# Batches 1 and 2 take the last batch's split of pairs between the engines in a state-space scan

## What is computed

```python
u = silu(conv(x) + conv_b)
delta = softplus(dt_proj_w @ dt_lo + dt_proj_b)
def step(state, xs):
    d_t, B_t, C_t, u_t = xs
    dA = jnp.exp(d_t[..., None] * A)
    state = state * dA + (d_t * u_t)[..., None] * B_t[:, None, :]
    y_t = jnp.einsum('ben,bn->be', state, C_t)
    return (state, y_t)
y = (y + D * u) * silu(z)
```

## Time and profile before

| | us |
|---|---|
| median of 3 runs | 533.96 (533.24 to 534.74) |
| profiled execution | 533.53 |
| its span | 531.8 |
| phases 0 to 3 begin | 27.9, 52.5, 79.7, 106.9 |
| phases 4 to 7 begin | 132.9, 161.2, 188.6, 219.7 |
| phases 8 to 11 begin | 249.8, 279.3, 306.9, 337.1 |
| phases 12 to 19 | 365.4 to 505.9 |

### The profile page before, as it was taken

How to read it: one execution, slowest core, us unless ns; L and a number is a source line. 1 busy time by engine, 2 the same in 40 slices (tenths; PEclk the granted TensorE clock), 3 DMA queues, 4 the chain that set the end, 5 groups by cost and what they waited for, 6 DMA issues and landing times.

```text
span 531.8 us, 9178 instructions
## 1 busy us (share of the span) xinstructions
PE 491.4 (92%) x3018; PEld 368.0 (69%) x3018; DVE 462.9 (87%) x846; ACT 380.1 (71%) x699; POOL 451.9 (85%) x327
## 2 busy tenths in 40 slices
PE   9989899998787999999999999999899999899688
PEld 5568788687676676668676777767566766676654
DVE  3799799799799999799999999798988989999852
ACT  4698848775876777866958776957868869768542
POOL 1389999959999999989999999889799898888910
PEclk9969799999999999999999999999999999999899
DMA  5595000126520001065230000077100000000001
GB/s 127 176 375 217 0 2 1 41 85 213 182 80 1 1 1 60 1 229 202 71 101 2 20 1 22 8 281 227 45 21 1 22 20 17 6 21 21 2 20 39
DMA packets 18704, 39.36 MB, mean 74 GB/s; under 512 B 5585, under 2 KB 6353, under 8 KB 18658
## 3 DMA queue, kind: packets, MB, share of 16 engines
q1 hardware_dynamic: 18658, 38.79, 21.4%
HBM read 34.33 MB, written 4.46 MB: 73 GB/s over the span
## 4 chain that ended last, share of the span: by engine, by line
PE 48%; POOL 19%; DVE 13%; ACT 10%; issue 9%; DMA 1%; DVEq 0%; SPq 0%; POOLq 0%; ACTq 0%
PE p_s L759 12%; PE p_y L781 11%; POOL state L586 9%; POOL dbu L571 7%; DVE state L1267 6%; PE p_v L814 5%; PE p_f L805 5%; PE p_tr L728 3%; PE p_v L691 2%; ACT da L1016 2%; DVE x L1216 2%; PE p_pr L703 2%; ACT pair_b L1000 1%; PE p_f L794 1%; PE p_pr L682 1%
## 5 line engine op out<-in xcount | busy, mean ns | idle before, releaser
L586 POOL TENSOR_TENSOR state<-state,c_bc 128x1024 f32<-128x1024 f32 (+1 forms) x131 | 256.7, 1970 | 21.6 <-DVE state L1267 19.2
L759 PEld LDWEIGHTS p_s<-pair_b,du_t 128*128 128x128 f32 x1072 | 140.7, 200 | 44.9 <-issue 33.4
L759 PE MATMUL p_s<-pair_b,du_t 128*128 128x128 f32 x1072 | 154.6, 287 | 16.0 <-DVE state L1267 15.8
L781 PE MATMUL p_y<-ident,state 128*128 128x128 f32 x1024 | 149.3, 276 | 0.0
L1016 ACT ACTIVATE p_s<-delta,a_neg 128x512 f32<-128x512 f32 (+1 forms) x162 | 93.7, 583 | 77.6 <-DVE state L1267 44.1
L1267 DVE TENSOR_TENSOR_SCAN state<-da,p_s 128x512 f32<-128x512 f32 (+1 forms) x116 | 134.5, 1172 | 16.0 <-PE p_s L759 13.1
L571 POOL TENSOR_TENSOR dbu<-du,pair_b 128x1024 f32<-128x1024 f32 (+1 forms) x80 | 145.3, 1819 | 0.2 <-DMA pair_b<-bc_rows 0.2
L781 PEld LDWEIGHTS p_y<-ident,state 128*128 128x128 f32 x1024 | 121.5, 144 | 23.3 <-issue 20.2
L1016 ACT ACTIVATE da<-delta,a_neg 128x512 f32<-128x512 f32 (+1 forms) x158 | 99.3, 647 | 18.5 <-DVE state L1267 18.4
L1267 DVE TENSOR_TENSOR_SCAN state<-p_s,dbu 128x512 f32<-128x512 f32 (+1 forms) x100 | 97.6, 996 | 7.6 <-POOL dbu L571 6.0
L805 PE MATMUL p_f<-u_sb,h_t 128*128 128x512 f32 x112 | 55.4, 597 | 2.4 <-DVE gw L1364 2.4
(11 more groups left out here) (175 smaller groups left out, 640.6 us busy)
## 6 DMA issues: line engine op xcount, KB each, us to landing
c_bc<-bc_rows SPq DMA_DIRECT2D x32, 512.0 KB, 5.1
pair_b<-bc_rows SPq DMA_DIRECT2D x16, 512.0 KB, 5.5
xs<-in_x SPq DMA_DIRECT2D x16, 256.0 KB, 4.6
out<-ot SPq DMA_DIRECT2D x14, 256.0 KB, 2.0
cx<-in_ctx_t SPq DMA_DIRECT2D x4, 512.0 KB, 3.8
u_sb<-in_u_w SPq DMA_DIRECT2D x1, 1024.0 KB, 14.1
v_sb<-in_v_w SPq DMA_DIRECT2D x1, 1024.0 KB, 15.6
w_in<-in_in_w_t SPq DMA_DIRECT2D x1, 384.0 KB, 4.7
```

The lines of the kernel that those rows point to most:

```text
L586: eng.tensor_tensor(pair, pair, c_bc[:, 2 * p:2 * p + 2, c0:c0 + w], ALU.mult).then_inc(po_cs, 1)
L759: mm = eng.matmul(p_s[g % BANKS][:, t * P:(t + 1) * P], du_t[:, f % 2, t, :], diagonals_of(n // 2)[:, n % 2, c0 // P + t, :], start=(t == ...
L781: mm = eng.matmul(p_y[:, t, :], slot(NS * f + n)[:, t * P:(t + 1) * P], ident[:, :], is_transpose=True, start=False, stop=(n == NS - 1 and ...
```

## The change

`POOL_SETS` gives batches 1 and 2 the set of batch 3: POOL makes dt\*u\*B of pairs 0, 2, 3, 5 and 6, and PE of pairs 1, 4 and 7, where POOL had 1, 3, 5, 7 and PE 0, 2, 4, 6. In `PAIRS_BY_DVE`, DVE multiplies by C the pairs 1 and 4 in all phases from 4 on. Before, these were the phases from 12 on, with pair 1 in phases 3 to 11 and pair 5 in phases 3, 7 and 11. In phases 1 and 2 DVE now takes pair 1, where it had none; in phase 3 it takes none, where it had pairs 1 and 5.

```diff
-POOL_SETS = [[2, 5], [1, 3, 5, 7], [1, 3, 5, 7], [0, 2, 3, 5, 6]]
+POOL_SETS = [[2, 5]] + 3 * [[0, 2, 3, 5, 6]]
...
     PAIRS_BY_DVE = [(LAST, 7)]
-    PAIRS_BY_DVE += [(f, p) for f in range(SPLIT, F) for p in (1, 4)]
-    PAIRS_BY_DVE += [(f, 1) for f in range(Q - 1, SPLIT)] + [(f, 5) for f in range(Q - 1, SPLIT, Q)]
+    PAIRS_BY_DVE += [(f, p) for f in range(Q, F) for p in (1, 4)]
+    PAIRS_BY_DVE += [(f, 1) for f in (1, 2)]
```

## The result

The changed kernel takes 545.08 us (median, 544.17 to 545.49) where the kernel before takes 533.60 us on the same chip. The ratio is 1.021 (95% interval 1.0187 to 1.0233): 11.5 us slower. The forecast was +5.8 us, 539.8 us, with a range up to 544.5.

A forecast was written before the change was run, and what follows sets the result against it. POOL was full in phases 4 and 5; PE, POOL and DVE nearly full in 6 to 11, with PE carrying the chain. Phase 6 begins 8.3 us late, phases 6 to 11 give -2.5: +5.8, 539.8 us; range 532.5 to 544.5.

The forecast's parts named there:

- the first turn: Phase 3 into 4: POOL's queue of 30.7 us starts pair 3 of phase 4 at 149.4 us, 5.5 us later.
- phases 1 and 2: DVE's added 1.37 us in each delays PE and ACT with nothing to cover it: +2.7 us, bounds 0 and +4.
- phases 6, 9, 10: Lengths set by the fullest engine: PE 28.8 us, DVE 28.6 us and DVE 28.6 us; -2.8 us.
- phases 7 and 8: Lengths set by the fullest engine: POOL 30.8 us in 7, DVE 29.4 us in 8; +0.5 us.
- phase 11: Length set by POOL at 28.1 us, two of its products being half size; -0.2 us.
- Each goes by the fullest engine: Phases 6 to 11: each lasts as long as its largest engine load, 174.3 us against 176.8 us, -2.5 us.
- Phases 12 to 19 keep their work: The phases after the changed split: work unchanged, so no cost was counted, 0 us.
- (c): Rival: longer waits drop TensorE's clock to 1.2 GHz, also in phase 8, 1.5 us a fall; 544.3 us, chance 0.19.
- The signs: POOL's queue into phase 4 lasts 30 to 31 us, DVE waits 4 or more there, phase 5 takes 28.5 or more.
- (a): Rival: PE decides in phases 6 to 11, giving 6.2 us; DVE's idle swallows early cost; 530.7 us, chance 0.14.
- (b): Rival: no difference, early costs of 2.9 and 1.4 us, gains of 4 in phases 6 to 11; 534.3, chance 0.12.
- (d): Rival: PE was no bound, so phases 6 to 11 give nothing; +8.3 us, 542.3 us, chance 0.10.

The follow-up runs named there:

- e2: Changed kernel with phases 1 to 3 as before: DVE has no C product in phases 1 and 2, pairs 1 and 5 in phase 3; 541.5 us.
- e1: Changed kernel with POOL's dt*u*B of the set's third pair moved ahead of C of pair 0, from phase 4 on; 535.9 us.
- e12: Changed kernel with POOL's C product of pair 5 only 64 of 512 columns wide in phases 3, 7 and 11; 541.1 us.
- e4: Only the change's second half: DVE's C products of the changed kernel with the old split of dt*u*B; 542.9 us.
- e7: Changed kernel with DVE's C product of pair 4 cut to 32 of 512 columns in phases 4 to 11; 540.7 us.
- e3: Only the change's first half: the new POOL sets in batches 1 and 2, with DVE's C products of before; 545.1 us.
- e11: Changed kernel with 27 extra matmuls on TensorE in phase 4 to fill its waits; 546.1 us.
- e6: Changed kernel with phases 1 to 3 as before, DVE also taking C of pair 5 in phases 7 and 11, and e1's move; 533.7 us.
- e10: e6 with DVE taking C of pairs 1 and 5 only in phases 7 and 11, not of 4 too; 530.5 us.

## Why the prediction was wrong, step by step

The sum had the right sign and the right mechanism at the first turn, and came to half of the loss. Per term, from the two profiled executions (+11.7 us in all):

| term | forecast, us | measured, us | |
|---|---|---|---|
| before phase 1 | 0 | +0.5 | not the change |
| phases 1 and 2 | +2.7 | +2.6 | right in number, in part by luck |
| phases 3 and 4 | +4.2 | +4.1 | right |
| phase 5 | +1.4 | +1.8 | near |
| phases 6, 9, 10 | -2.8 | -1.6 | size |
| phases 7 and 8 | +0.5 | +3.3 | **failed** |
| phase 11 | -0.2 | -1.1 | size |
| phases 12 to 19 | 0 | +2.2 | **failed** |

**The first turn went by the working.** Pair 3 of phase 4 was to start at 149.4 us and starts at 149.82; POOL's run to it from phase 3's third product was to take 30.7 us, and takes from 119.1 to 149.8 us. The forecast rested on counting POOL's queue between two named instructions. In phases 1 and 2 the pair put in costs more than was said: without it they take 2.7 and 1.2 us less (e2). The +2.6 us of the table are met because the kernel before had the lower clock (0.87) in phase 1 of its profiled execution. Against the 26.2 us of the other versions without the pair, the two phases cost 3.5 us. In phase 5 the mean share fell from 1.00 to 0.94; e1, at 1.00, takes 1.0 us more than before there, where the sum had 1.4.

**The step that failed is "Each goes by the fullest engine", and with it "Phases 12 to 19 keep their work".** For phases 7 and 8 the first gave 30.8 + 29.4 = 60.2 us; they take 62.9. POOL's 30.8 us of phase 7 didn't make phase 7 long (29.9 us): it ran over into phase 8, where DVE, with 29.3 us of its own, had to wait 2.90 us for pair 3. This is the stall of phase 4 once more, with the same cause, the same place in POOL's order and the same instruction waiting. I had worked it out in full for the first turn and had even named phase 8 under rival (c), as TensorE's matter, and still summed phases 7 and 8 as if the engines could swap their slack within a phase. The maximum over engines is a floor for a phase, not its length: the time at which POOL's queue delivers the pair that DVE waits for decides. The third turn was left out altogether: the work of phases 12 to 19 is the same, but POOL enters phase 12 late (a wait of 2.61 us), +1.9 us. e12 confirms the cause at all three turns, since 2 us less on POOL shorten phases 4, 8 and 12 by 1.6 to 2.0 us each, and e1 does it by order alone.

**In phases 6 and 10** TensorE was full before and its relief was real: they are 1.9 and 1.2 us shorter. e4 shows it with DVE's products in place and the old sets: PE is busy for 30.1 and 29.7 us there, the phases take 30.1 us, and the changed kernel has 29.1. The forecast lacked 0.3 and 0.5 us, because DVE (28.3 us) and POOL's order (28.5 us in e7) lie close together and come to 29.1 between them: in phase 6 POOL waits 1.20 us for a scan, and DVE 0.63 us for a product of POOL. e1 moves the product and gets 28.4. Phase 9, where PE was not full before (25.9 of 27.6 us), lacked 0.4 us. That goes with the clock: it takes 28.4 us at 1.00 (e1 and e4). In phase 11 POOL's load was put too high, at 28.1 us; it is busy for 26.3 us, and the phase takes 27.2.

**The signs.** Nearly all that were to show the forecast right came true (POOL's run of 30.7 us, the wait of 4.59 us, phase 5 at 29.2 us, phases 6 and 10 at 29.1 us; phase 7, at 29.9 us, just not), and the forecast was wrong all the same. None of them looked at phases 8 and 12.

**The rivals.** (a) fell: phases 6 to 11 give nothing in sum (+0.6 us rather than -6.2), and e3, where DVE's added work is absent, isn't faster (though POOL has 12 products a phase in it, so that e3 alone would not decide). (b) fell with the measured +11.5. (c), TensorE's clock, came nearest in number, 544.3 us, but not by its working. It was right about a deeper fall in phase 4 and wrong about its price: the mean share fell from 0.94 to 0.79 there, and e11, which holds it at 0.95, gains nothing. The fall that it saw coming in phase 8 is not there (1.00); it comes in phases 5 and 9 (0.94). There it does seem to reach the path: the length of phase 9 goes 28.4, 29.0, 30.4 and 31.4 us at mean shares of 1.00, 0.94, 0.89 and 0.85 (e1, changed, e12, e2), with the same work in all four, and the other order of e1 is not the reason, since e6 and e10 have it and take 29.0 us at 0.94. By these rows I estimate 1.3 us for phases 5 and 9 of the changed kernel, from 29.2 and 29.0 us against e1's 28.4 in both. No run held the clock up in them, so this rests on the rows agreeing and not on an experiment. (d), 542.3 us, fell by its reason. Had TensorE not been the bound, phases 6 and 10 would not have shrunk; what made phases 6 to 11 give nothing is the turn in their middle, since with the same TensorE work they take 173.1 us in e1 and 173.9 in e10, against 176.8 before. The page that (d) cited (the Trainium skill, Trainium Kernel Development and Optimization, "Performance Expectations") holds the busy share of the weight loads for a good measure of how close a kernel is to its roofline. That share was 69% in phase 6 before (21.4 of 31.1 us), and less work on PE made the phase shorter all the same.

**The range** ended at 544.5 us. It had no room for a second and a third stall like the first. Phases 8 and 12 took 3.5 and 1.9 us more than before; that 5.4 us, added to the forecast of 539.8, gives 545.2, just past its end.

Phase 8 of e6 and e10 is still 30 us, where DVE's busy time would allow 29.1 to 29.3. Of this, 0.5 us are DVE's wait for ACT's `p_f`, which stands in the kernel before as well.

**What stays open**: what makes the clock fall in phase 9 of one version and not of another; and what the clock is worth in phases 5 and 9 by an experiment. Of each version only one execution is profiled.

## What to carry to other kernels

Where engines work through orders written by hand, a change that leaves an engine's sum unchanged can still cost: find the consumer that waits, and count the producer's queue between the last instruction that was on time and the one waited for. Do this at every place where the pattern recurs, and never price a phase by its fullest engine alone when a neighbouring phase loads another engine. And put what another engine waits for ahead of what nobody needs yet: moving one product by one place made the changed kernel 9.2 us faster, and the kernel before 3.3 us (0.6%).

## What the runs showed of the hardware

TensorE's clock fell to 1.2 GHz in phase 4 of the changed kernel during a wait of 2.32 us, which came after one of 1.99 us and a short burst. Neither is as long as the 2.67 us of the earlier trace rows. It was still at 1.2 GHz after the next wait, of 2.20 us, and up to about 157 us; the eight records of a dt\*u\*B tile took 1.92 and 2.08 us in this stretch. From PE's timeline, and the granted clock in windows (as a share of 2.4 GHz):

```profile
140.59 0.66 PE L781 MATMUL p_y<-ident,state 128*128 128x128 f32 x4 [1.99 <-POOL state L586]
...
145.21 1.97 PE L781 MATMUL p_y<-ident,state 128*128 128x128 f32 x8 [2.32 <-POOL state L586]
146.97 1.92 PE L759 MATMUL p_s<-pair_b,du_t 128*128 128x128 f32 x8
151.09 2.08 PE L759 MATMUL p_s<-pair_b,du_t 128*128 128x128 f32 x8 [2.20 <-DVE state L1267]
```

```profile
139.00:142.00 3.00, 1.41 (x6) 0.71 (x6) 2.41 (x3) 1.76 (x4) 3.00 (x2) 1.00 0.14 34
142.00:145.00 3.00, 0.89 (x5) 0.42 (x4) 2.11 (x2) 2.12 (x6) 3.00 (x2) 0.71 0.42 141
145.00:148.00 3.00, 2.79 (x13) 2.79 (x14) 0.23 (x1) 3.00 (x7) 3.00 (x3) 0.50 0.45 173
...
157.00:160.00 3.00, 3.00 (x28) 2.92 (x28) 3.00 (x6) 2.61 (x5) 2.83 (x2) 1.00 0.76 244
```

A product on POOL keeps its price beside a busier DVE: 2.35 or 2.36 us for dt\*u\*B in the rows above, as in the earlier trace rows. The Trainium skill (GPSIMD Engine Reference, "3.1 Elementwise — side-by-side cycle accounting") gives 4497 ns for an fp32 tensor_tensor of 2048 elements, 2.2 ns an element; here 2361 ns for 1024 are 2.3 ns an element, and the trace agrees within 5%.
